# Sliding-window transformer block on 8 cores: the attention stage's value products issued two tiles later, and its first ring loads issued at the stage's own start

## What is computed

```python
x = x + _L0_attn_ref(_layernorm(x, axis=-1), Wq, Wk, Wv, Wo)
x = x + _L0_ffn_ref(_layernorm(x, axis=-1), W0, bias0, W1, bias1)

# attention, n = block of 512 queries; it sees its own block and the one before
kw = jnp.concatenate([k_prev, kb], axis=3)
vw = jnp.concatenate([v_prev, vb], axis=3)
scores = jnp.einsum('bhnid,bhnjd->bhnij', qb, kw) * scale
base = (j > i) & (j <= i + WIN)          # WIN = 512
scores = jnp.where(mask[None, None], scores, -jnp.inf)
attn = jax.nn.softmax(scores, axis=-1)
out = jnp.einsum('bhnij,bhnjd->bhnid', attn, vw)
```

## Time and profile before

| | us |
|---|---|
| median of 2 timed runs | 3844.17 (3842.16 to 3846.19) |
| the profiled execution, time | 3858.99 |
| its span, slowest core (core 1), first to last instruction | 3857.4 |
| spans of the 8 cores | 3819.2 to 3857.4 |
| mean granted TensorE clock, by core | 0.937 to 0.941 of full |

### The profile page before, as it was taken

One profiled execution on the slowest core, in us unless ns is written; L12 is line 12 of the kernel. 1 busy time (PEld: TensorE's weight loads), 2 busy tenths in 40 slices (PEclk: granted clock), 3 DMA queues, 4 the chain that ended last, 5 costly groups with the idle time before them and its releaser, 6 DMA issues. The chain is left out here.

```text
span 3857.4 us, 47231 instructions; the slowest of 8 cores (3819.2 to 3857.4 us)
## 1 busy us (share of the span) xinstructions
PE 3276.6 (85%) x17600; PEld 1631.6 (42%) x17600; DVE 785.4 (20%) x1618; ACT 787.4 (20%) x1285; POOL 592.9 (15%) x933
## 2 busy tenths in 40 slices
PE   1599999997367576666659999999998998999999
PEld 1344444443244443535334444444443443444444
DVE  5555554000043434444320000000000000000000
ACT  3355554111342332324101111111110000000000
POOL 1000101001300000000010000003004333433321
PEclk9999999999588888888869999999998999999999
DMA  9322555552954133150282333334618989989774
GB/s 235 104 58 63 98 102 104 97 100 73 291 100 153 66 113 107 39 180 1 99 175 55 71 82 82 82 82 86 122 40 217 217 187 206 220 221 224 193 197 126
DMA packets 191858, 488.96 MB, mean 127 GB/s; under 512 B 21776, under 2 KB 54544, under 8 KB 188816
## 3 DMA queue, kind: packets, MB, share of 16 engines
q0 software_dynamic: 132304, 304.97, 38.3%
q1 hardware_dynamic: 59328, 180.97, 14.3%
HBM read 487.96 MB, written 115.34 MB: 156 GB/s over the span
## 5 line engine op out<-in xcount | busy, mean ns | idle before, releaser
L1204 PE MATMUL pool<-w1q,gq 128*128 128x512 bf16 x4096 | 903.8, 382 | 49.1 <-DMA gq<-g_sp 49.1
L1059 PE MATMUL pool<-ln2T,w0b 128*128 128x512 bf16 x4096 | 886.2, 380 | 2.2 <-SPq L120 2.2
L370 PE MATMUL pool<-ln1T,wbuf 128*128 128x512 bf16 x3584 | 776.6, 379 | 6.6 <-PE pool L370 4.6
L1204 PEld LDWEIGHTS pool<-w1q,gq 128*128 128x128 bf16 x4096 | 397.7, 98 | 539.0 <-issue 75.9
L1059 PEld LDWEIGHTS pool<-ln2T,w0b 128*128 128x128 bf16 x4096 | 401.2, 98 | 487.0 <-issue 5.1
L370 PEld LDWEIGHTS pool<-ln1T,wbuf 128*128 128x128 bf16 x3584 | 350.3, 98 | 432.7 <-issue 12.9
L144 DVE TENSOR_TENSOR obuf<-pool,yh 128x512 f32<-128x512 f32 x64 | 44.3, 692 | 1813.6 <-PE pool L1208 1646.6
L1135 POOL DMA_DIRECT2D gq<-g_sp x256 | 225.4, 900 | 767.6 <-PE pool L1208 569.7
L170 ACT ACTIVATE gst<-pool,bias_s 128x2048 bf16<-128x2048 f32 x64 | 126.0, 1969 | 745.0 <-PE pool L1059 745.0
L795 PE MATMUL pool<-wo_sb,outT 128*128 128x512 bf16 x1024 | 238.7, 397 | 33.8 <-DVE ybuf L899 29.8
L824 ACT ACTIVATE expb<-pool 128x640 bf16<-128x640 f32 x256 | 180.6, 707 | 276.9 <-PE pool L738 271.6
(11 more groups left out here) (59 smaller groups left out, 1924.1 us busy)
## 6 DMA issues: line engine op xcount, KB each, us to landing
gq<-g_sp POOLq DMA_DIRECT2D x256, 512.0 KB, 12.9
w0b<-w_t POOLq DMA_DIRECT2D x128, 256.0 KB, 16.6
g_sp<-gst SPq DMA_DIRECT2D x64, 512.0 KB, 2.7
w1q<-w_t POOLq DMA_DIRECT2D x256, 128.0 KB, 20.5
xb<-x_ctx SPq DMA_DIRECT2D x20, 1024.0 KB, 11.3
wbuf<-wk_t POOLq DMA_DIRECT2D x64, 256.0 KB, 16.6
wbuf<-wv_t POOLq DMA_DIRECT2D x64, 256.0 KB, 17.4
kring<-k_sp POOLq DMA_DIRECT2D x16, 1024.0 KB, 12.2
```

The costliest lines, as they stand in the source:

```text
L370: ins = tn.matmul(pool[:, slot * 2048 + k * 512: slot * 2048 + (k + 1) * 512], lhs, ln1T[:, roff: roff + 512], start=(i == 0), stop=(i == ...
L1059: ins = tn.matmul(pool[:, slot * 2048 + scv * 512: slot * 2048 + (scv + 1) * 512], lhs, ln2T[:, i * TOWN + scv * 512: i * TOWN + (scv + 1) ...
L1204: tn.matmul(pp, lhs, w1q[hq4 % 2][:, n * 512: (n + 1) * 512], start=(n == 0), stop=False)
```

## The change

There are two edits.

**First**, PE's value products of a head are issued two steps later. Before, PV stands behind T of the head's fourth tile. In the changed kernel it is issued at step s for the head whose fourth tile is s-4, behind T(s-2) of that step. The loop over steps runs to 68 instead of 66, so that the last head's PV is still issued. Its waits and its 20 matmuls are the same.

**Second**, the mask and the ring loads of block 0 are no longer issued in the v stage. They stand at the start of POOL's list in the attention stage, behind the barrier and ahead of the loads of wo_sb. The rings and the mask are allocated inside the attention stage. Within every block's ring loads the order is now k, v, q instead of k, q, v.

```diff
@@ v stage, POOL @@
-                        g.dma_start(msk[:], msk_in).then_inc(sem["sMsk"], 16)
-                        ring_kq(g, 0)
-                        g.wait_ge(sem["sSpVa"], 16 * 4)
-                        g.wait_ge(sem["sSpVb"], 16 * 4)
-                        ring_v(g, 0)
@@ attention stage, POOL @@
                     barrier(g)
-                    if not DO_V:
-                        g.dma_start(msk[:], msk_in).then_inc(sem["sMsk"], 16)
-                        ring_kq(g, 0)
-                        ring_v(g, 0)
+                    g.dma_start(msk[:], msk_in).then_inc(sem["sMsk"], 16)
...
+                    def rings(qb):
...
+                    rings(0)
                     for i0 in range(0, 16, 4):
                         g.dma_start(
...
                     for qb in range(1, NQB):
                         g.wait_ge(sem["sQbPE"], qb)
-                        ring_kq(g, qb)
-                        ring_v(g, qb)
+                        rings(qb)
@@ attention stage, PE @@
-                        for step in range(66):
+                        for step in range(68):
...
                             tst = step - 2
-                            if tst >= 0:
+                            if 0 <= tst < 64:
...
-                                if qc == 3:
-                                    gidx = qb * 16 + hh
-                                    tn.wait_ge(sem["sExpT"],
-                                               eidx(qb, hh, 3) + 1)
+                            pvi = step - 4
+                            if pvi >= 0 and pvi % 4 == 3:
+                                hh = pvi // 4
+                                gidx = qb * 16 + hh
+                                tn.wait_ge(sem["sExpT"],
+                                           eidx(qb, hh, 3) + 1)
```

More of the change, by code:

```diff
@@ L503, in _ @@
                         s.wait_ge(sem["sSpQb"], 16 * (NP1_G // 2))
[L505 to L534, removed]
         if DO_V:
@@ L621, in build_nc @@
         with p2:
+            kring = p2.enter_context(nc.sbuf_tensor("kring", [128, 16 * 1024], BF16))
+            vring = p2.enter_context(nc.sbuf_tensor("vring", [128, 8 * 2048], BF16))
+            qring = p2.enter_context(nc.sbuf_tensor("qring", [128, 16 * 512], BF16))
             wo_sb = p2.enter_context(nc.sbuf_tensor("wo_sb", [128, 16 * 2048], BF16))
+            msk = p2.enter_context(nc.sbuf_tensor("msk_s", [128, 5 * 640], BF16))
             expb = [p2.enter_context(nc.sbuf_tensor(f"expb{j}", [128, 640], BF16))
@@ L690, in _ @@
                     barrier(g)
-                    if not DO_V:
-                        g.dma_start(msk[:], msk_in).then_inc(sem["sMsk"], 16)
-                        ring_kq(g, 0)
-                        ring_v(g, 0)
+                    g.dma_start(msk[:], msk_in).then_inc(sem["sMsk"], 16)
+                    k_spv = k_sp.rearrange("(o p) t -> p o t", p=128)
+                    v_spv = v_sp.rearrange("(s p) f -> p s f", p=128)
+                    q_spv = q_sp.rearrange("(o p) t -> p o t", p=128)
                     wo_tv = wo_t.rearrange("(i p) f -> p i f", p=128)
+                    def rings(qb):
+                        for o0 in range(0, 16, 4):
+                            g.dma_start(
+                                kring[:, o0 * 1024:(o0 + 4) * 1024].rearrange(
+                                    "p (o c) -> p o c", c=1024),
+                                k_spv[:, o0: o0 + 4,
+                                      qb * 512: qb * 512 + 1024]
+                            ).then_inc(sem["sRing"], 16)
+                        for j0 in range(0, 8, 2):
+                            g.dma_start(
+                                vring[:, j0 * 2048:(j0 + 2) * 2048].rearrange(
+                                    "p (j f) -> p j f", f=2048),
+                                v_spv[:, qb * 4 + j0: qb * 4 + j0 + 2, :]
+                            ).then_inc(sem["sRing"], 16)
+                        for o0 in range(0, 16, 8):
+                            g.dma_start(
+                                qring[:, o0 * 512:(o0 + 8) * 512].rearrange(
+                                    "p (o c) -> p o c", c=512),
+                                q_spv[:, o0: o0 + 8, qb * 512:(qb + 1) * 512]
+                            ).then_inc(sem["sRing"], 16)
+                    rings(0)
                     for i0 in range(0, 16, 4):
@@ L757, in _ @@
                                 ins.then_inc(sem["sTpE"], 1)
-                                if qc == 3:
-                                    gidx = qb * 16 + hh
-                                    tn.wait_ge(sem["sExpT"],
-                                               eidx(qb, hh, 3) + 1)
[L762 to L776, removed]
-                                    ins.then_inc(sem["sPV"], 1)
@@ new lines, in _ @@
+                            pvi = step - 4
[4 more added lines that the diff above has]
+                                           eidx(qb, hh, 3) + 1)
+                                if gidx >= 2:
+                                    tn.wait_ge(sem["sOutT"], gidx - 1)
+                                pv = ppv[gidx % 2]
+                                ins = None
+                                for qx in range(4):
+                                    for jc in range(qx, qx + 5):
+                                        vt = vring[:, jc * 2048 + hh * 128:
+                                                   jc * 2048 + (hh + 1) * 128]
+                                        col = qx * 512 + jc * 128
+                                        ins = tn.matmul(
+                                            pv[:, qx * 128:(qx + 1) * 128],
+                                            vt,
+                                            expT[hh % 2][:, col: col + 128],
+                                            start=(jc == qx),
+                                            stop=(jc == qx + 4))
+                                ins.then_inc(sem["sPV"], 1)
@@ L931, in _ @@
                             v.sig(sem["sNmr"])
-        p2o.close()
         if MAX_PHASE < 3:
```

## The result

The changed kernel took 3707.15 us at the median, the kernel before 3848.18 us in the same runs. The ratio is 0.9609, with a 95% interval from 0.9586 to 0.9631: 150 us less, of which 128 were forecast.

A forecast was written before the change was run, and what follows sets the result against it. A chain passing from engine to engine bounds each attention head, the clock second. Chain -116, clock -20 and ring loads +8 make -128 us, from 3844.17 to 3716; own range 3690 to 3745, 8 in 10 from 3680 to 3762.

The forecast's parts named there:

- The sum for edit 1: Attention heads: seven links between engines give 5.31 us a head instead of 7.24, 116 us less over 60 periods.
- The cast ahead of exp(c0): On ACT: the cast waits for PV and delays the first exp of the second head after by 0.07 us.
- The clock term: Attention blocks: 40 us beyond full-clock heads, from lower clock and block 0's wide masks; half, 20 us, taken as gain.
- the last head of each block: Attention blocks: the last period gives a little more, as PV stands ahead of the last transposes; left out.
- everything between the blocks: Program outside the two edits, Wo part included: instructions and waits taken as unchanged, with no gain or loss.
- The ring loads: Start of attention: loads behind the barrier take 40.0 us at 309 GB/s; PE starts near 1072 instead of 1064.6, +8 us.
- The v stage's tail: End of the v stage without the loads: 20th copy at about 1025.2, attention stage starting at about 1031.
- the loads had slowed the v stage: V stage: its last stores shared DMA engines with the early loads, so moving them is mostly no addition.
- the clock dips vanish: Rival for the attention heads: denser PE stays at 2.4 GHz, 40 us instead of 20, so 3696 us; chance 0.15.
- The shorter chain of three tiles: Rival for the attention heads: three tiles in flight set the pace, 4.6 us a head, 3664 us; chance 0.12.
- Bare loads: Rival at the v stage's end: its length stays, loads cost 40 us, links 0.1 longer, 3800 us; chance 0.08.
- a slower kernel: Rival for the attention heads: only two tiles in flight, 7.5 us a head, lower clock, 3952 us; chance 0.02.

The follow-up runs named there:

- the copy first: Changed kernel with DVE's copy into expT put ahead of rec and scaling of a later tile; head 4.97 us against 5.26, no comparable time of the whole.
- the groups of five with the later cast: Changed kernel with a head's 20 value matmuls cut into four groups, one per query tile, and ACT's cast behind a later exp: 3625.98 us, one execution.
- kernel with fillers: Kernel before, with 28 matmuls that add nothing to the result put into PE's wait ahead of each head's value products: ratio 0.9834 to the kernel before.
- edit 1 alone: Kernel before with only the value products issued two steps later, ring loads left in the v stage: ratio 0.9576 to the kernel before, median 3699.82 us.

## Why the prediction was right

**The mechanism and its size.** The sum for edit 1 was 1.93 us a head, from links of the trace before. The links measured after are 1.12, 0.74, 0.97, 0.97, 1.19 and 0.28: 5.27 against 5.31 forecast, 1.97 us a head and 118 us over 60 periods against 116. The cast ahead of exp(c0), estimated at 0.07, is 0.04. That the chain is this one is shown by three runs which change parts of it and move the head by nearly what the chain says: one step instead of two (6.22 for 6.04), the copy first (4.97 for 4.87), the groups of five with the later cast (4.32 for 4.2 to 4.3).

**The clock term was undersized.** The forecast took 20 of 40 us, half, "since density of this size has not decided it so far". All of it went: the blocks are at 1.00, and 474.7 - 312.0 = 163 us are 118 for the chain and 45 more. Of these the last head of each block gives 8 (3.3 us instead of 5.3, which the forecast mentioned and left out); some 37 are the lower clock that is gone, less the wide masks of block 0, which stayed (5.38 us a head there). So the term that was mis-sized is the clock, 20 put down and some 37 measured. The step behind it was to compare two heads of the kernel before, one at 1.00 and one at 0.80, and to conclude that density does not decide. Both had the same work and the same 1.85 us of standing; they show that a head like that can run at either clock, and say nothing of a head without the standing. The kernel with fillers shows that: with PE at work through the wait, 0.98 to 1.00 outside the odd second block. Whether it is the standing in one piece that counts, or the busy time as a whole, stays open. The Trainium skill, page "TensorE: Matmul & The Clock Gate", section "Part 1: The HAM clock gate", says that the gate follows how busy the array has been. The trace agrees with the page: 1.00 in all four blocks of the changed kernel. The forecast cited it and kept half.

**One term was not there.** The forecast left everything between the blocks as it was; it became 12 us shorter (8 and 4 in the ledger). Most of that is the clock again: in these rows a Wo part starts at once at the full level when the heads ahead of it were at it. The first 128 Wo matmuls of blocks 0 and 1 before, and of block 0 after:

```profile
1198.11 30.30 PE L795 MATMUL pool<-wo_sb,outT 128*128 128x512 bf16 x128 [0.93 <-ACT outT L812]
...
1412.42 30.66 PE L795 MATMUL pool<-wo_sb,outT 128*128 128x512 bf16 x128 [1.03 <-ACT outT L812]
```

```profile
1169.64 27.79 PE L787 MATMUL pool<-wo_sb,outT 128*128 128x512 bf16 x128 [0.93 <-ACT outT L804]
```

After the change they take 27.79 us in each of the four blocks of this core; before they took 30.30, 30.66, 27.79 and 30.62, so 8 of the 12 us are there. The kernel with fillers agrees: its ring loads are those of before, and between its blocks it is 7 us shorter. The new order of the loads is not the cause, for with edit 1 alone the time between the blocks is that of the changed kernel (287 and 286 us, medians over the cores, against 297). The other 4 us differ from core to core and were not taken apart.

**The ring loads.** Forecast +8, measured +11 to +12 at PE's start. The load itself was read well: 41 us at 308 GB/s, against 40 at 309. The v stage's tail was not: its last copy started at 1028.9 us instead of 1025.2, and the next stage at 1034.3 instead of 1031. A v_sp store took 4.3 us at the median of the 20, where the forecast put 2.6, from the y_sp stores. The claim that the loads had slowed the v stage, and that moving them is mostly a move, holds: without them the v stage ended some 30 us earlier, and 42 us of loading came behind it.

**The rivals.** That the clock dips vanish, given 0.15, is what happened, on top of the forecast's chain. Its time, 3696 us, is nearer to the 150 us measured (3694 from the same 3844) than the forecast's own 3716. The shorter chain of three tiles did not come until the value products were cut into groups. Bare loads and a slower kernel did not come.

In sum the forecast's 128 us lacked 2 of the chain, 25 of the clock and the blocks' ends, 12 between the blocks, and had 4 too few for the loads: 163 at the end of the stage, of which the last stage's scatter hides 9 in the profiled execution. So the chain carries the result, and the number came out low because the clock, there and between the blocks, was given too little.

## What to carry to other kernels

When engines hand tiles to each other in a ring, walk the ring in the timeline link by link and ask for each wait whether the thing waited for is the tile's own work or another tile's, standing ahead in some engine's order; here one group of instructions, moved by two steps, gave 118 us with every instruction as it was. Work that has to be done once a head fitted here in the gaps, in pieces (4.32 us a head), better than in one block on the ring (5.23). A stall in the middle of TensorE's work was paid twice here, in its own time and in a lower clock. The loads that were issued early were not free, for the v stage ended 30 us later with them; they still let PE start 11 us earlier.

## What was not expected of the hardware

Filling a wait with useless matmuls made a kernel faster by 1.7% (0.9834), with 10% more matmuls in the program.

In that same run, two of eight cores (2 and 3) went through the whole second block at a granted clock of 0.81, most heads alike, 7.52 us instead of 7.12. It is no mixture of the full level and the half one, for the fillers and the value matmuls are both longer, by 15 to 16%. The fillers and the value group of one head there:

```profile
1303.82 2.01 PE L764 MATMUL ppv<-idm_s 128*128 128x128 bf16 x28
...
1305.81 1.47 PE L775 MATMUL ppv<-expT,vring 128*128 128x128 bf16 x20
```

28 fillers took 2.01 us against 1.73 in the third block, and 20 value matmuls 1.47 against 1.28. The Trainium skill, page "TensorE: Matmul & The Clock Gate", section "Seeing it yourself", tells of a current limit that sets the clock to 13/16, 0.81, for a whole die. The number agrees; the whole die does not, for here two cores of a die were at it, while the other two showed 0.98 to 1.00 in all four blocks. The same two cores showed it in the same block in the kernel with edit 1 alone (0.81, and 316 us for the four blocks instead of 312), which ran on the same chip. What sets it off, and why only in that block, stays open; the changed kernel's own profile has it on no core.

The head of the kernel with fillers at full clock is 7.12 us, 0.12 shorter than the clean head before. PV starts 0.63 us behind the start of the copy that it waits for, where it was 0.74. The cause is the wait on sOutT: in the kernel before, PV passes it behind the wait on the copy, from the third head on; in the kernel with fillers it is passed ahead of them. The first head of the kernel before has no such wait:

```profile
1075.61 0.49 DVE L866 COPY expT<-ptp 128x640 bf16<-128x640 bf16 x1
...
1076.24 1.70 PE L771 MATMUL ppv<-expT,vring 128*128 128x128 bf16 x20 [2.04 <-DVE expT L866]
```

That is 0.63 us, after 2.04 us of standing, so it does not matter whether PE has just been working. The second head has 0.63 too, and the other 62 have 0.73 or more. A wait that was over long ago, but stands behind the one that ends last, cost 0.11 us here each time.
